# A graph network of one GAT stage and three attention layers: contexts in column strips, and the attention contexts behind the scores

## What is computed

```python
# GAT stage, per sample; D = 384, N = 256, 12 heads of 32
h = einsum('bnd,ade->bane', x, W); th = tanh(h)
attn = th @ w_src + (th @ w_dst).T                 # leaky relu 0.2, mask by adj
feat = elu(softmax(attn) @ h + b)
gate = sigmoid(x @ H_w.T + H_b)
x = layernorm(x + gate * feat + (1 - gate) * x)
# three layers, 6 heads of 64
q, k, v = heads(x @ Wq + bq), heads(x @ Wk + bk), heads(x @ Wv + bv)
probs = softmax(q @ k.T / 8 + bias_of(adj))
ctx = probs @ v
x = layernorm(x + ctx @ Wf + bf)
```

## Time and profile before

| | |
|---|---|
| median of 3 runs | 3695.76 us (3695.51 to 3696.64) |
| profiled execution, its own time | 3700.19 us |
| its span | 3698.0 us |
| granted clock of PE, mean | 0.963 |
| busy: PE, DVE, ACT, POOL | 90%, 81%, 73%, 34% |
| PE matmuls in the trace | 25312 |

### The profile page before, as it was taken

One profiled execution on the slowest core, in us unless ns is written; L12 is line 12 of the kernel. 1 busy time (PEld: TensorE's weight loads), 2 busy tenths in 40 slices (PEclk: granted clock), 3 DMA queues, 4 the chain that ended last, 5 costly groups with the idle time before them and its releaser, 6 DMA issues. The chain is left out here.

```text
span 3698.0 us, 86729 instructions
## 1 busy us (share of the span) xinstructions
PE 3340.8 (90%) x25312; PEld 3070.1 (83%) x25312; DVE 3002.3 (81%) x9529; ACT 2706.1 (73%) x7923; POOL 1270.9 (34%) x1384
## 2 busy tenths in 40 slices
PE   7999999999996998998997998998997999898997
PEld 6989898889885888887886888888886888888886
DVE  5887788778875888888886888887886888887887
ACT  5888888888884776776775776776775777676775
POOL 1333333333332433333332343433333243333433
PEclk9999999999997999999998999999998999999998
DMA  1000000000001101111111010101111011111100
GB/s 66 29 20 29 30 29 20 29 30 29 20 19 60 38 30 38 34 34 35 33 38 57 29 38 31 38 29 39 33 35 34 25 38 35 34 34 34 37 31 27
DMA packets 107320, 124.52 MB, mean 34 GB/s; under 512 B 39824, under 2 KB 106320, under 8 KB 106320
## 3 DMA queue, kind: packets, MB, share of 16 engines
...
## 5 line engine op out<-in xcount | busy, mean ns | idle before, releaser
L758 POOL TENSOR_TENSOR a_residual<-a_x,a_br 128x384 f32<-128x384 f32 x192 | 208.8, 1110 | 1452.5 <-DVE a_mix L923 1434.9
L843 ACT ACTIVATE a_probs<-a_logits,a_nmax 128x256 f32<-128x256 f32 x1152 | 571.1, 498 | 34.6 <-DVE a_nmax L945 17.6
L945 DVE CUSTOM_DVE_ANT_0 a_logits<-a_s,a_mask 128x256 f32<-128x256 f32 x1152 | 438.6, 417 | 154.8 <-PE a_s L1039 90.9
L73 PE MATMUL a_pj<-a_xt_hi,a_w_lo 128*128 128x256 f32 x1728 | 524.6, 304 | 9.1 <-DVE a_xt_lo L888 9.1
L74 PE MATMUL a_pj<-a_xt_lo,a_w_hi 128*128 128x256 f32 x1728 | 513.6, 297 | 0.0
L75 PE MATMUL a_pj<-a_xt_hi,a_w_hi 128*128 128x256 f32 x1728 | 513.6, 297 | 0.0
L1068 PE MATMUL a_pt<-a_ident,a_probs 128*128 128x128 f32 x2304 | 355.6, 277 | 160.0 <-DVE a_probs L902 160.0
L854 ACT ACTIVATE a_pt_hi<-a_pt 128x512 fp32r<-128x512 f32 x576 | 341.7, 593 | 150.9 <-PE a_pt L1068 150.7
L1068 PEld LDWEIGHTS a_pt<-a_ident,a_probs 128*128 128x128 f32 x2304 | 271.7, 142 | 190.5 <-DVE a_probs L902 183.1
L451 DVE CUSTOM_DVE_ANT_0 g_v<-g_z,g_v 128x256 f32<-128x256 f32 x768 | 291.9, 417 | 143.0 <-ACT g_v L343 134.0
L1081 PE MATMUL a_cx<-a_pt_lo,a_v_split 128*128 128x256 f32 x1152 | 352.9, 329 | 49.3 <-DVE a_pt_lo L973 48.9
...
## 6 DMA issues: line engine op xcount, KB each, us to landing
...
```

Source lines behind the costliest of these rows:

```text
L73: pe.matmul(out, a[1], b[0], start=first, stop=False)
L843: last = act.activation(probs[:, i, t, :], logits[:, h % 2, t, :], ACT.Exp, scale=-1.0, bias=nmax[:, u, h, t:t + 1], accum_out=sums[:, u, ...
L945: last = dve.tensor_tensor_reduce(out=logits[:, j % 2, t, :], in0=s_ps[j % 2][:, t, :], in1=mask[u][:, t, :], scale=-HEAD_DIM ** -0.5, sca ...
```

## The change

**In both stages** the context is made from plain F32 operands, without a split: one matmul per head and half of the keys where two were, with the stationary operand only as wide as the head (64 or 32 columns, `v_sb`, `h_sb`), and written to the rows of PSUM that belong to that head. Heads stand side by side in strips of columns of the array: two in attention (`pair_of_contexts`), four in the GAT stage (`four_contexts`). So a block is made for two or four heads at once, when the last of them is evicted. `pt_hi` and `pt_lo` go; `pt_sb` takes a plain copy, by ACT for even heads and by DVE for odd ones, each with its own semaphore (`pt_even_read`, `pt_odd_read`).

**Attention.** V is only copied (L796): no high and low part, nothing on POOL. The context comes out whole, so `moved` and `ct` go; ACT makes `ct_hi` straight from PSUM and DVE `ct_lo`, in one step, step j for the pair whose odd head is j-4. On DVE `ct_lo` stands behind `normalise` and ahead of `lo_of_step`. On PE the block of contexts stands right behind the scores of steps 0, 2 and 4.

**GAT.** H is only copied. `C_LAG` goes from 4 to 3, blocks stand in steps 2, 6 and 10 behind the transposes. Three evictions into `ct` instead of six; `make_back` is 3 transposes per half in place of 6 matmuls with `fold`.

```diff
+            def pair_of_contexts(half, u, last_head):
+                c = last_head // 2
+                pe.wait_ge(pt_even_read, evictions(half, u, last_head - 1))
+                pe.wait_ge(pt_odd_read, evictions(half, u, last_head))
+                pe.wait_ge(v_read, at(NT, half, u, NT))
+                pe.wait_ge(ct_split, at(DC, half, u, c - 1))
+                for kt in range(NT):
+                    for s in range(2):
+                        h = 2 * c + s
+                        last = pe.matmul(cx_ps[(DC * u + c) % 2][rows_of(s), 0:N], v_sb[u][:, kt, h * HEAD_DIM:(h + 1) * HEAD_DIM], pt_sb[:, pt_slot(u, h), kt, :],
+                                         start=kt == 0, stop=kt == NT - 1)
+                last.then_inc(contexts, 1)
```

```diff
@@ attention, PE @@
                         pe.wait_ge(maxed, at(HEADS, half, u, j))
                         pair_of_scores(u, j // 2)
+                    head = behind(cur, prev, HEADS, j, C_LAG)
+                    if head and head[2] % 2 == 1:
+                        pair_of_contexts(*head)
                     if nxt and j in PLAN:
                         make_step(*nxt, PLAN[j], prev)
...
-                    if head := behind(cur, prev, HEADS, j, C_LAG):
-                        half, u, h = head
-                        c = h // 2
-                        pe.wait_ge(pt_split, at(HEADS, half, u, h + 1))
...
-                        for kt in range(NT):
-                            for part in (pt_lo, pt_hi):
-                                last = pe.matmul(cx_ps[(3 * u + c) % 2][:, cols], v_split_sb[u][:, kt, h, :], part[:, h % 2, kt, :],
@@ attention, ACT @@
+                    if head and head[2] % 2 == 0:
                         half, u, h = head
                         act.wait_ge(transposed, at(HEADS, half, u, h + 1))
-                        act.wait_ge(contexts, at(HEADS, half, u, h - 1))
-                        act.activation(pt_hi[:, h % 2], pt_ps[h % 2][:, :, :], ACT.Identity).then_inc(pt_hi_done, 1)
+                        act.wait_ge(contexts, at(DC, half, u, h // 2 - 1))
+                        act.activation(pt_sb[:, pt_slot(u, h)], pt_ps[0][:, :, :], ACT.Identity).then_inc(pt_even_read, 1)
                     head = behind(cur, prev, HEADS, j, C_LAG + 1)
                     if head and head[2] % 2 == 1:
...
-                        act.wait_ge(ct_added, at(DC, half, u, c + 1))
+                        act.wait_ge(contexts, at(DC, half, u, c + 1))
                         act.wait_ge(back_made, at(NT, half, u, 0))
-                        act.activation(ct_hi[:, c, :], ct[:, :], ACT.Identity, bias=bc[:, V, c:c + 1]).then_inc(ct_hi_done, 1)
...
-                        for s in range(2):
-                            last = act.activation(moved[rows_of(s), :], cx_ps[(3 * u + c) % 2][rows_of(1 - s), s * N:(s + 1) * N], ACT.Identity)
-                        last.then_inc(ct_moved, 1)
...
+                        act.activation(ct_hi[:, c, :], cx_ps[(DC * u + c) % 2][:, 0:N], ACT.Identity, bias=bc[:, V, c:c + 1]).then_inc(ct_hi_done, 1)
@@ attention, DVE @@
                     pair = behind(cur, prev, HEADS, j, C_LAG + 1)
...
-                        dve.wait_ge(ct_moved, at(DC, half, u, c + 1))
...
-                            last = dve.tensor_tensor(ct[rows, :], cx_ps[(3 * u + c) % 2][rows, s * N:(s + 1) * N], moved[rows, :], ALU.add)
+                        dve.wait_ge(ct_hi_done, at(DC, half, u, c + 1))
+                        dve.scalar_tensor_tensor(ct_lo[:, c, :], cx_ps[(DC * u + c) % 2][:, 0:N], bc[:, V, c:c + 1], f32(ct_hi[:, c, :]),
+                                                 ALU.add, ALU.subtract).then_inc(ct_split, 1)
                     if nxt and PLAN.get(j, VS) < VS:
                         lo_of_step(*nxt, PLAN[j])
...
-                        dve.wait_ge(pt_hi_done, at(HEADS, half, u, h + 1))
-                        dve.tensor_tensor(pt_lo[:, h % 2], pt_ps[h % 2][:, :, :], f32(pt_hi[:, h % 2]), ALU.subtract).then_inc(pt_split, 1)
-                    if pair:
...
-                        dve.scalar_tensor_tensor(ct_lo[:, c, :], ct[:, :], bc[:, V, c:c + 1], f32(ct_hi[:, c, :]), ALU.add, ALU.subtract).then_inc(ct_split, 1)
+                        dve.wait_ge(transposed, at(HEADS, half, u, h + 1))
+                        dve.wait_ge(contexts, at(DC, half, u, h // 2 - 1))
+                        dve.tensor_copy(pt_sb[:, pt_slot(u, h)], pt_ps[1][:, :, :]).then_inc(pt_odd_read, 1)
@@ GAT, PE @@
+                pe.wait_ge(pt_even_read, evictions(half, u, last_head - 1))
+                pe.wait_ge(pt_odd_read, evictions(half, u, last_head))
+                pe.wait_ge(ctx_read, at(GROUPS, half, u, g - 1))
+                for kt in range(NT):
+                    for i in range(QUAD):
+                        h = g * QUAD + i
+                        cols = slice(h * GAT_DIM, (h + 1) * GAT_DIM)
+                        last = pe.matmul(cx_ps[(GROUPS * u + g) % 2][i * GAT_DIM:(i + 1) * GAT_DIM, 0:N], h_sb[u][:, kt, cols], pt_sb[:, pt_slot(u, h), kt, :],
+                                         start=kt == 0, stop=kt == NT - 1)
-                for c in range(GROUPS):
-                    last = pe.matmul(back_bank[:, c * 2 * GAT_DIM:(c + 1) * 2 * GAT_DIM], ct[u][:, c, t * P:(t + 1) * P], fold[:, :], start=True, stop=True)
+                for g in range(GROUPS):
+                    last = pe.transpose(back_bank[:, g * P:(g + 1) * P], ct[u][:, g, t * P:(t + 1) * P], ident[:, :])
```

More of the change, by code:

```diff
@@ L186, in reads, with evictions, pt_slot @@
             return at(len(READ_STEPS), half, u, READ_STEPS[k])
+        def evictions(half, u, h):
+            return at(GAT_HEADS // 2, half, u, h // 2 + 1)
+        def pt_slot(u, h):
+            return (GAT_HEADS * u + h) % PT_BUFS
         def pj_bank(k):
@@ L555, in slot @@
                         last.then_inc(transposed, 1)
-                    if head := behind(cur, prev, GAT_HEADS, j, C_LAG):
-                        half, u, h = head
-                        c = h // 2
-                        pe.wait_ge(pt_split, at(GAT_HEADS, half, u, h + 1))
-                        if h % 2 == 0:
-                            pe.wait_ge(ctx_read, at(GROUPS, half, u, c - 1))
-                        for kt in range(NT):
-                            for part in (pt_lo, pt_hi):
-                                last = pe.matmul(cx_ps[c % 2][:, 0:N], h_split[u][:, kt, h, :], part[:, h % 3, kt, :],
-                                                 start=h % 2 == 0 and kt == 0 and part is pt_lo,
-                                                 stop=h % 2 == 1 and kt == NT - 1 and part is pt_hi)
-                        last.then_inc(contexts, 1)
+                    head = behind(cur, prev, GAT_HEADS, j, C_LAG)
+                    if head and head[2] % QUAD == QUAD - 1:
+                        four_contexts(*head)
                     if prev and j in BACK_PLAN:
                         make_back(*prev, BACK_PLAN[j], cur, nxt)
-            pe.wait_ge(consts_loaded, 7 * 16)
+            pe.wait_ge(consts_loaded, 6 * 16)
             pe.wait_ge(consts_ready, 1)
@@ L584, in attention_phase @@
     Q, K, V, O = range(4)
+    PT_BUFS = 4
     with ExitStack() as ctx:
@@ L669, in back_bank, with evictions, pt_slot @@
             return pj_ps[(u + 1 + BACK_AT + t) % 2]
-        def v_parts(u, t, s):
-            return [v_split_sb[u][:, t, s::2, half * HEAD_DIM:(half + 1) * HEAD_DIM] for half in (s, 1 - s)]
+        def evictions(half, u, h):
+            return at(HEADS // 2, half, u, h // 2 + 1)
+        def pt_slot(u, h):
+            return (HEADS * u + h) % PT_BUFS
         def rows_of(s):
@@ L800, in _ @@
         def _(act):
-            start(act, pj_hi, v_read, v_hi_done, exped, pt_hi_done, ct_moved, ct_hi_done)
+            start(act, pj_hi, v_read, exped, pt_even_read, ct_hi_done)
             def copy_v(half, u, t):
                 act.wait_ge(pj_made, step(half, u, VS + t) + 1)
-                act.wait_ge(v_split, at(NT, half, u, 0))
-                act.activation(v[:, t, :], pj_bank(u, VS + t)[:, 0:D], ACT.Identity).then_inc(v_read, 1)
-            def hi_of_v(half, u, t):
-                act.wait_ge(v_read, at(NT, half, u, t + 1))
-                src = v[:, t, :].rearrange("p (h two d) -> p h two d", two=2, d=HEAD_DIM)
-                for s in range(2):
-                    last = act.activation(v_parts(u, t, s)[0], src[:, :, s, :], ACT.Identity)
-                last.then_inc(v_hi_done, 1)
+                act.wait_ge(contexts, at(DC, half, u, -DC))
+                act.activation(v_sb[u][:, t, :], pj_bank(u, VS + t)[:, 0:D], ACT.Identity).then_inc(v_read, 1)
             def hi_of_step(half, u, k):
@@ L1069, in slot @@
                         last.then_inc(transposed, 1)
-                    if head := behind(cur, prev, HEADS, j, C_LAG):
-                        half, u, h = head
-                        c = h // 2
-                        pe.wait_ge(pt_split, at(HEADS, half, u, h + 1))
```

(10 more changed lines are left out.)

156 lines of the change are left out of this document (63 added, 93 removed).

## The result

| | before | changed |
|---|---|---|
| median | 3696.16 us (3695.51 to 3696.64) | 3783.16 us (3780.39 to 3787.72) |
| ratio | | 1.0237 (1.0219 to 1.0254) |
| profiled execution, its span | 3698.0 us | 3778.6 us |
| granted clock, mean | 0.963 | 0.949 |

The change makes the kernel 87 us slower. The forecast was 10 us faster; the time lies inside the range, on the other side.

What follows compares the result with a forecast made beforehand. PE was taken as nearly full in the graph stage; in attention, PE's work plus waits on DVE. Graph -91, attention +88, ends -8 made -11 us on 3700: 3689, as a median 3686 us; range 3580 to 3790 us.

Steps and rivals of the forecast that it cites:

- The price of a block: Context block on PE, both stages: 2 x 0.427 = 0.853 us with strips fully overlapping, plus 0.09 to 0.18 at its ends.
- The rival with strips one behind the other: Context blocks cost 1.71 us in attention and 3.41 in the graph stage; about 4115 us in all; chance 0.13.
- overlap in part: Context strips overlap only in part, blocks of 1.07 us; 3766 us, sharing chance 0.22 with a clock fall in every sample.
- Wait (1): Attention step 4: PE's contexts of heads 0 and 1 wait 2.1 us per sample for DVE's copy of head 1.
- Wait (2): Attention step 1: PE's projections wait for `a_xt_lo` of the next sample; 1.3 us together with 0.4 for `a_probs`.
- The sample: Attention sample: 25.4 us by adding up one round, +0.85; +0.95 taken, over 93 steady samples +88 us.
- The clock: Attention: clock falls after PE's waits stay as before, 0.7 us per sample; never falling gives -60 us, always +75.
- always +75 us: Attention: the cost if the clock fell in every sample, where the forecast kept the falls as before.
- a rival of 0.22: Strips overlap in part, or the clock falls in every attention sample: 3686 + 80 = 3766 us; chance 0.22.
- The graph stage: GAT stage, 32 samples: PE work -3.2 us each, -2.85 taken since DVE sets the pace in heads 7 to 9; -91 us.
- The ends: Layer ends and graph stage's end: ACT's move and DVE's add leave the chain through the contexts; -8 us in all.

Runs made afterwards that it cites:

- filler: The changed kernel with 14 useless F32R matmuls of 256 columns on PE ahead of the context block of attention step 4 and its wait: 3646.05 us, ratio 0.9857.
- gate_later_copy: Changed kernel; in GAT, ACT's first gate tanh goes behind the next head's exponentials, DVE's step 9 copy ahead of ELU and gate: 3746.76 us, ratio 1.0121.
- gat_only: The changed GAT stage with the attention layers of the kernel before: 3630.07 us, ratio 0.9818 to the kernel before.

## Why the prediction was wrong

It had the size of PE's work and nearly that of the new waits in attention. It took the wrong value for what the wait does to the clock, and left out the waits of the graph stage.

- *The price of a block: right.* 0.43 us per matmul, strips side by side; 1.00 to 1.02 us in all where I had 0.94 to 1.03. The rival with strips one behind the other (4115 us) falls, and so does overlap in part: with the 0.09 to 0.18 us at its ends such a block would have taken 1.17 us or more. The 1.08 us was my estimate by the Trainium skill (TensorE: Matmul & The Clock Gate, Part 3), whose 2.38 for three column tiles is 0.79 of full overlap. The trace lies nearer to full overlap: two strips hold 1.73 us of work in 1.02, a factor of 1.7 or 0.85 of full overlap, with entering and leaving counted. No run here has three strips.
- *Wait (1): right, 2.1 us forecast, 2.14 measured.* The chain, from the last matmul at 2203.36: ACT at +0.32, `a_ct_hi` at +0.73 behind that (ACT's next start, 2204.41), `a_ct_lo` +0.51, `a_qk_lo` +0.40, copy +0.78, PE +1.03 (forecast 0.32, 0.71, 0.54, 0.40, 0.79, 0.81).
- *Wait (2): smaller.* 0.7 us for `a_xt_lo` and next to nothing for `a_probs`, where I had 1.3 together (0.4 of it for `a_probs`, whose waits are 3.3 us in the whole kernel).
- *The sample: right.* 25.4 by adding up, 25.5 taken; measured 25.6, and 25.45 with the clock held up by `filler`. Against 24.55 us before without a fall that is +0.9 us, and 93 x 0.9 = 84 us where I had 88. Two misses of size cancel in it, which is luck: waiting came to 2.9 us where I had 3.4, and a block behind the scores takes 1.01 to 1.02 us where I had 0.94.
- *The clock: the step that failed.* "Neither is clearly better; I keep the 0.7 us per sample." Before, falls cost 25.17 - 24.55 = 0.6 us per sample; after, 26.93 - 25.45 = 1.5 us. The sample before without a fall is the 24.55 of the earlier trace rows; `filler` puts the whole of the falls after at 137 us. By 93 samples it is about 80 us more than before, the "always +75 us" that I had named and put under a rival of 0.22. Before, the longest wait of a steady sample was 1.30 us and 0.48 followed it, with a fall in under half of the samples; now it is one of 2.14 us, with a fall in about eight of nine (64 of the 72 samples between turns). That it is longer than the one before, and whole, stood in my own sum. How long a wait has to be for the clock to fall, these runs don't show.
- *The graph stage: the second step that failed.* -91 us forecast, -40 measured. The work was sized about rightly, the waits were not. Between the turns a sample went from 33.4 to 31.9 us (the 33.5 of the earlier trace rows takes in the longer samples at the turns). From 100 to 1060 us PE waited 25 us before and 87 after, about 2.1 us more per sample; so its work fell by some 3.5 us, an estimate from these rows, where I had 3.2. `gate_later_copy` brings the sample to 30.9 us, 2.5 less than before, and the stage then brings 40 + 43 = 83 us. The prediction says of DVE in heads 7 to 9 that "there it will set the pace for a while", and yet the sum takes only 0.35 us off for it. I had added up DVE's work and not asked who waits for its last instruction in step 9: the block of four heads in step 10 does. That is the part that runs show; the waits for the division (4.7 us before, 20.5 after) and for the exponentials (0.6 and 15.5) grew too, stay in `gate_later_copy` (21.6 and 15.9), and what would remove them was not tried.
- *The ends: -8 forecast, about -40.* Between turns of the loop a sample grew by 1.76 us, and 72 of those are 127 us; yet the stretch of 94 samples grew by 131 only. The samples at the loop's turns and between layers hardly grew (674.1 us in place of 670.0 over eleven pairs). I took 93 samples times the steady value. Some 10 us of that lie at the six turns, 191 us before and 192 after: DVE's pause there, shown above under "Each stage alone", got shorter. My own had it, a wait of 6.1 us for `a_probs` where a steady sample shows 1.30, and I did not ask where it lay. The rest lies where layers begin and end; what covers the wait and the falls there was not tried.

In sum: -40 + 84 + 80 - 40 = +84 us, and 87 were measured. Of these four, the wait and the ends are read from traces; the GAT term is the difference of two runs, and the clock term is read from the samples, with `filler` beside it for what the falls cost after.

## What to carry to other kernels

When a block is put right behind something short, work out the wait in front of it and then ask what its length does to the clock: one wait of 2 us per sample (162 us in all) cost here almost as much again in slow matmuls behind it (137 us). A loss of this kind has a cheap test, filler work in the wait: if that makes the kernel faster, the wait has a second price. And in a queue written out by hand, look at which instruction releases another engine and put it ahead of work that nobody waits for: three such moves, on PE, DVE and ACT, turned a loss of 2.4% into a gain of 7.7%.

## What the runs showed of the chip

- F32 matmuls in two column strips run side by side whatever their order: a block with both matmuls of a strip in a row takes the same 1.02 us as one that alternates, and six matmuls, four of them in one strip, take 0.86 us more than four.
- Idle time of PE can be worth filling with matmuls that compute nothing (137 us here).
- The same attention code took 29 us less behind another GAT stage, half of it where its loop turns, at a pause of DVE in which it waits for nothing that the profile shows (5.6 to 6.3 us at each turn before, at most 4.4 in `gat_only`). No run here tells why.
